# Middle stage of an audio tower kernel: dense products before every channel group, a third set of systems moved to the last stage, four stores moved to another queue

## What is computed

```python
# T: rows 0, 2, 4, ... of each segment of 256 rows -> 3 blocks of 128 tokens per sequence, attention in the block
scores = q @ k.T / 16;  h = softmax(scores) @ v            # q = k = v = the rows
# A: delta rule attention, 4 heads of 64, on h normalised
q, k, v = silu(conv4(x @ Wq)), silu(conv4(x @ Wk)), silu(conv4(x @ Wv))
T = inv(I + tril(kb @ k.T, -1))                            # unit triangular system per chunk
o_delta = chunkwise delta rule with T
fir_short, fir_long = causal filters of 3 and 63 taps over v, each channel with its own taps
o = gate-weighted mixture of fir_short, fir_long, o_delta and v;  h += rmsnorm(o) @ Wo
# F: 6 experts, 2 chosen per token by a router
h += sum_e weight_e * (gelu(LN(h) @ w1_e) @ w2_e)
```

## Time and profile before

| what | value |
|---|---|
| timed runs | median 2389.22 us of 3 (2379.17 to 2395.04) |
| the profiled execution | 2393.8 us, span from first to last instruction 2392.1 us |
| TensorE, VectorE, ScalarE, GpSimd busy | 94%, 77%, 54%, 23% of the span |
| mean granted clock of TensorE | 0.973 of full |
| steps of the last stage, one starting after the other | 47.53 us, with two columns solved in them or none |

### The profile page before, as it was taken

The page is one execution under the profiler, slowest core; times in us unless marked ns, Lnnn a source line. Parts: engine busy times, 40 slices in busy tenths (PEclk is TensorE's granted clock), DMA queues, the critical chain, the costliest instruction groups (busy, mean ns, idle before and its releaser), DMA issues.

```text
span 2392.1 us, 53303 instructions
## 1 busy us (share of the span) xinstructions
PE 2251.9 (94%) x20796; PEld 1635.1 (68%) x20796; DVE 1852.8 (77%) x5111; ACT 1290.8 (54%) x2632; POOL 555.5 (23%) x413
## 2 busy tenths in 40 slices
PE   5999999999799779999999999999999999999997
PEld 4666666666587666777677767776776677767765
DVE  4999999999868367677778777777777667767765
ACT  4888888888624334544454455445544544454452
POOL 1444444444400011121112111111111121112111
PEclk9999999999958879999999999999999999999999
DMA  3776777777778912233224222322233224222300
GB/s 98 231 245 229 229 241 245 236 238 236 247 241 314 378 60 71 71 108 96 78 70 139 91 77 71 125 81 74 70 132 105 71 70 133 77 71 76 125 21 21
DMA packets 224297, 334.44 MB, mean 140 GB/s; under 512 B 113870, under 2 KB 190766, under 8 KB 215342
## 3 DMA queue, kind: packets, MB, share of 16 engines
q1 hardware_dynamic: 219726, 309.01, 39.1%
q10 hardware_dynamic: 2304, 12.58, 1.3%
q0 software_dynamic: 2016, 9.44, 1.0%
HBM read 191.66 MB, written 164.23 MB: 149 GB/s over the span
## 4 chain that ended last, share of the span: by engine, by line
PE 49%; DVE 7%; ACT 6%; issue 4%; POOL 0%; DVEq 0%
PE bank L1662 7%; PE bank L1672 7%; PE bank L1595 6%; PE bank L1475 4%; PE bank L1555 4%; PE bank L1632 4%; PE bank L1571 2%; PE bank L1507 2%; PE bank L1543 2%; ACT L1808 2%; ACT L1803 2%; DVE v_all L2111 1%; PE bank L1503 1%; PE bank L1485 1%; DVE DL L2019 1%
## 5 line engine op out<-in xcount | busy, mean ns | idle before, releaser
L2111 DVE SCALAR_TENSOR_TENSOR v_all<-bank,we,v_all 128x256 f32<-128x256 f32 x576 | 264.9, 476 | 219.3 <-PE bank L1672 214.3
L739 DVE SCALAR_TENSOR_TENSOR Y<-bank,convw,Y 128x383 f32<-128x383 f32 (+2 forms) x576 | 330.6, 602 | 3.2 <-ACT Y L627 2.9
L1672 PE MATMUL bank<-w2e,HE 128*128 128x256 f32 x1152 | 327.9, 395 | 2.4 <-DVE v_all L2111 2.3
L1662 PE MATMUL bank<-v_all,w1e 128*128 128x384 f32 x768 | 289.6, 500 | 2.4 <-ACT HE L1808 2.3
L445 PE MATMUL bank<-pb,wqkv 128*128 128x384 f32 x768 | 282.4, 491 | 1.8 <-DVE Y L739 1.8
L1672 PEld LDWEIGHTS bank<-w2e,HE 128*128 128x128 f32 x1152 | 198.0, 191 | 55.3 <-issue 19.3
L1808 ACT ACTIVATE HE<-bank 128x384 f32<-128x384 f32 x192 | 94.1, 490 | 248.9 <-PE bank L1662 248.2
L1595 PE MATMUL bank<-v_all,w1g 128*128 128x384 f32 x512 | 193.4, 500 | 2.0
L1662 PEld LDWEIGHTS bank<-v_all,w1e 128*128 128x128 f32 x768 | 134.5, 191 | 75.9 <-issue 19.8
L445 PEld LDWEIGHTS bank<-pb,wqkv 128*128 128x128 f32 x768 | 132.1, 191 | 61.1 <-DVE Y L739 8.3
L1786 ACT ACTIVATE first_stage<-bank 32x384 f32<-32x384 f32 (+1 forms) x192 | 92.2, 480 | 135.7 <-PE bank L1583 119.2
(11 more groups left out here) (217 smaller groups left out, 5199.1 us busy)
## 6 DMA issues: line engine op xcount, KB each, us to landing
packa<-pa SPq DMA_DIRECT2D x32, 1932.0 KB, 6.2
v_all<-packa SPq DMA_DIRECT2D x32, 1932.0 KB, 8.1
packb<-pb SPq DMA_DIRECT2D x32, 768.0 KB, 6.1
v_all<-packb SPq DMA_DIRECT2D x32, 768.0 KB, 10.8
toeplitz<-taps SPq DMA_DIRECT2D x128, 190.0 KB, 5.3
toep<-toeplitz SPq DMA_DIRECT2D x32, 760.0 KB, 7.6
packb<-fsk SPq DMA_DIRECT2D x32, 384.0 KB, 2.7
first_stage<-fl SPq DMA_DIRECT2D x32, 384.0 KB, 8.7
```

Source lines behind the costliest of these rows:

```text
L739: dve.scalar_tensor_tensor(out=Y[:, j, lag:T], in0=proj_bank[j][:, 0:T - lag], scalar=convw[:, j, CK - 1 - lag:CK - lag], in1=Y[:, j, lag: ...
L1662: mm = pe.matmul(bank[6][:, 0:T], w1e[:, a, k, :], YT[s][:, a, :], start=(a == 0), stop=(a == HALF - 1))
L1672: pe.matmul(expert_bank(b), HE[k % 2][:, b * P:(b + 1) * P], w2e[:, k, :], start=True, stop=True)\
L2111: dve.scalar_tensor_tensor(out=HA[s][:, b, :], in0=expert_bank(b), scalar=we[s][:, b, k:k + 1], in1=HA[s][:, b, :], op0=ALU.mult, op1=ALU. ...
```

## The change

The calls of `dense` in the middle stage are laid otherwise: three at the start, four in front of group 0 behind the wait for its tile, three before groups 8, 16 and 24 as before, and one before every other group, ahead of the wait for its tile. Set 2 of the systems is not begun in the middle stage; in the last stage one column is solved right behind the transposed diagonal and two behind the last statistics, for set 2 in steps 0 to 9 and for set 3 in steps 10 to 19. GpSimd's loads of set 3 no longer wait for steps of set 2. The four stores of the last 64 channels are issued by SyncE at the start of the last stage, not by ScalarE at the end of the middle one.

```diff
-SPLIT = 20
+SOLVE_PASSES = (SC - 2) // 3
@@ middle stage, tensor
-                dense(5)
+                dense(3)
                 for i in range(0, groups // NT):
                     for s in range(NT):
                         it = i * NT + s
-                        if it and it % GI == 0:
-                            dense(3)
+                        if it:
+                            dense(1 if it % GI else 3)
                         pe.wait_ge(*toep_loaded[s].now(i))
+                        if it == 0:
+                            dense(4)
@@ middle stage, scalar
-                act.wait_ge(*fl_copied.now(NH * GI - 1))
-                for q in range(FQ):
-                    store(NH - 1, q)
                 act.wait_ge(setup_act, CLEARED)
@@ middle stage, gpsimd
-                load(3, 0, 2 * SOLVE_STEPS + 9)
-                load(3, 1, 2 * SOLVE_STEPS + 17)
-                load(3, 2, 2 * SOLVE_STEPS + 25)
+                for part in range(SG):
+                    load(3, part)
@@ middle stage, vector
-                solve["begin"](dve, 2)
-                for j in range(1, SPLIT):
-                    solve["column"](dve, 2, j)
@@ last stage, sync
+                def store_filtered(g, q):
+                    part = NB * BLK * DH // FQ
+                    sp.dma_start(dram["fl"][g][:, q * part:(q + 1) * part], stage[g][:, q * part:(q + 1) * part])\
+                        .then_inc(fl_stored[g], 16)
+
+                sp.wait_ge(*tail["fl_copied"].now(D // 8 - 1))
+                for q in range(FQ):
+                    store_filtered(NH - 1, q)
                 sp.wait_ge(fl_stored[2], 16 * FQ)
@@ last stage, vector
-                def columns_of(n):
-
-                    if n < 6:
-                        at = SPLIT + min(3 * n, 5 + n)
-                        return 2, at, at + (3 if n < 2 else 2 if n == 2 else 1)
-                    at = 1 + 2 * (n - 6)
-                    return 3, at, at + 2
-
-                def solve_columns(n):
...
+                def solve_first(n):
+                    if n < 2 * SOLVE_PASSES:
+                        g, turn = 2 + n // SOLVE_PASSES, n % SOLVE_PASSES
+                        if turn == 0:
+                            solve_begin(dve, g)
+                        solve_column(dve, g, 1 + 3 * turn)
+
+                def solve_others(n):
+                    if n < 2 * SOLVE_PASSES:
+                        g, turn = 2 + n // SOLVE_PASSES, n % SOLVE_PASSES
+                        solve_column(dve, g, 2 + 3 * turn)
+                        solve_column(dve, g, 3 + 3 * turn)
@@ step
                         transpose_diagonal(n, n % 2, 0, 0, n // 2).then_inc(tdiag_ready.sem, 1)
+                        solve_first(n)
                     if 0 <= f < NB:
                         add_expert(f, 4, 0)
@@ step
                         input_stats(n, 5)
-                        solve_columns(n)
+                        solve_others(n)
```

More of the change, by code:

```diff
@@ L2113, in add_expert @@
                         .then_inc(acc_done.sem, 1)
-                def columns_of(n):
-                    if n < 6:
-                        at = SPLIT + min(3 * n, 5 + n)
-                        return 2, at, at + (3 if n < 2 else 2 if n == 2 else 1)
-                    at = 1 + 2 * (n - 6)
-                    return 3, at, at + 2
-                def solve_columns(n):
-                    if n > 20:
-                        return
-                    g, first, last = columns_of(n)
-                    if first == 1:
-                        solve_begin(dve, g)
-                    for j in range(first, last):
-                        solve_column(dve, g, j)
+                def solve_first(n):
[9 more added lines that the diff above has]
+                        solve_column(dve, g, 3 + 3 * turn)
                 def step(i):
```

## The result

The changed kernel takes 2389.59 us (median of 20 runs, 2383.44 to 2396.75), the kernel before, timed beside it, 2378.89 (20 runs, 2375.91 to 2398.78). So two things were off: before is some 10 us faster than those three runs said, and the change makes it slower instead of faster. The profiled execution after took 2391.9 us (span 2390.2), the one before 2393.8 (2392.1): profile against profile the change looks 1.9 us faster. That contradiction is what this study is about.

The account below looks back on a forecast made before the run. The prediction took TensorE at half clock to bound the middle stage. Its terms, -4.0 (TensorE's end) - 4.4 (stage end) + 1.3 (solves) - 1.5 (step 0 clock) = -8.6 us, took 2389.2 to 2380.6; range 2366 to 2400.

Parts of the forecast that it names:

- Slow halves that go: Middle stage: 19 half groups and two triples of dense products return to full clock, -28.5 us.
- The change does less than it says: Rival, chance 0.06: the clock is not lost in every run before, so the median lands near 2389 us.
- The transfers end step 0: Rival, chance 0.14: full DMA engines land fl as before however early the meeting is, leaving 2387 us.
- Lost clock: Rival, chance 0.11: the clock falls in the first eight groups, single products do not raise it; +20, 2409 us.
- The start: Middle stage: four dense products behind the first load's wait are in the open, +4.9 us, bounds 3.4 and 6.7.
- The singles: Middle stage: one dense product ahead of every other group, 28 x 0.84 = +23.5 us on TensorE's path.
- Waits for loads: Middle stage: 5.9 us of later waits go and 2 us of new ones come, -3.9 us; the first load's 2.2 stay.
- TensorE's end: End of TensorE's middle-stage work: -4.0 us in sum, at 807.8 against 811.8 us.
- The end of the stage: Middle stage's end: four of ScalarE's five store issues move behind the engines' meeting, -4.4 us.
- cover of 3.0 us: Last stage's start: fl lands 17.8 us after the meeting, VectorE is free at 23.0, TensorE's first state comes at 26.0.
- Clock in step 0: Last stage's first step: after a shorter pause the clock stays up at first, -1.5 us, bounds 0 and -10.
- The solves: Last stage: 19 more columns on VectorE cost nothing except in step 2, +1.3 us, bounds 0 and 1.9.

Follow-up runs that it names:

- b_again: The kernel before, unchanged, run and profiled once more: 2381.65 us, ratio 1.0009.
- rest_only: The changed kernel with all dense products as before, so only the solves and the stores are moved: 2372.44 us, ratio 0.9981.
- stores_only: The kernel before with only the four last stores moved from ScalarE to SyncE, ahead of its loads: 2377.62 us, ratio 1.0016.
- x3_late: rest_only with GpSimd's three loads of the fourth systems group moved behind its first operation of the last stage: 2372.77 us, ratio 0.9963.
- rest_x3_fl: x3_late with SyncE's loads of fl ahead of those of the second chunk's packs and factors: 2368.1 us, ratio 0.9955.
- rest_step0: rest_only with three unused products behind the last group and five in the last stage's step 0: 2380.24 us, ratio 1.0006.
- after_fl: The changed kernel with SyncE's loads of fl first, no products in step 0: 2384.8 us, ratio 1.0039.
- the square: Four changed-kernel versions, fl behind packs and factors or first: 2389.6 and 2384.8 us without products in step 0, 2390.9 and 2381.5 with five.
- dense_only: The kernel before with only the change's dense products in the middle stage; solves and stores as before: 2390.87 us, ratio 1.0055.
- solves_only: The kernel before with only group 2 solved in the last stage and group 3's loads issued without waits: 2377.73 us, ratio 1.0009.
- after: The changed kernel itself, against the kernel before: 2389.59 us, ratio 1.0036.
- no_single: The changed kernel without the 28 single dense products, keeping the four behind the first wait: 2378.18 us, ratio 1.0.
- half_singles: The changed kernel with single dense products ahead of odd groups alone, 16 in place of 28: 2381.42 us, ratio 1.0024.
- nosingle_x3_fl_step0: The changed kernel without single products, fourth systems group loaded in the last stage, fl first, five products in step 0: 2370.45 us, ratio 0.9964.

## Why the prediction was wrong

**The step that failed is "Slow halves that go", -28.5 us.** Its arithmetic was right for the execution that was profiled, but that execution was a rare one. The sum also started from the median of three runs, 2389.2, where 20 runs give 2378.9. In b_again the part from the first dense product to the last Toeplitz product is 138.8 us and not 155.8. Its floor is 8.3 (start) + 32 x 3.31 + 3 x 2.52 = 121.8, and TensorE waited 6.0 for later loads; so half clock cost it 11.0 us, not 28.5. With that term the sum is -8.6 + 17.5 = +8.9, and the medians lie 10.7 apart (the profiled executions of the changed kernel and of b_again 6.4). Rest_only, stores_only, x3_late and rest_x3_fl have 130.4 to 131.6, so many executions lose less still. How often the long one comes: of 115 later runs of the kernel before, 16 were above 2389 us and 82 below 2380. Two profiles of such slow executions exist, the first one of before and rest_step0's, and both have the half clock through groups 0 to 7; the seven other profiles of kernels that start as before do not. That the others among the 16 have it too is argued, not shown. Their mean granted clock fits: 0.969 to 0.974, 0.9715 on average, where the 82 have 0.9802, which over 2385 us comes to some 41 us more at half clock (an estimate). But a mean does not say where: b_again's profile had 0.972 too, with its half clock elsewhere.

**Rivals.** "The change does less than it says", near 2389, is what happened as to its reason. That its number is met is luck: it meant no change against 2389.2, and what came is a loss of 10.7 against 2378.9. I gave it 0.06, though three runs 16 us apart, with the profiled one at the slow end of them, were in front of me. "The transfers end step 0" was right in that fl came too late, and wrong about why (below). "Lost clock" did not occur. The rule of the Trainium skill ("TensorE: Matmul & The Clock Gate", Part 1) would have put the sum at +12, close to the truth, but for another reason: the slow halves were mostly not there to be mended. Where the clock did fall at the start it stayed down for 48 us in both traces that show it, 45 of them unbroken Toeplitz work, against the rule; in rest_only it came back in such work (717.4 to 720.8), as the rule has it. So what the prediction read from one trace, that Toeplitz groups release nothing and dense products do, does not hold in every execution.

**What the products cost.** The start: +4.9 forecast, 5.0 measured, with the clock at half until 669.6, as assumed. The singles: 0.84 forecast, 0.81 measured. Waits for loads: 3.3 us in all, the first one alone, where 4.2 were expected. TensorE's end: 807.8 forecast, 806.8 measured (with a first product 1.6 us later than before's). So the changed kernel's middle stage was forecast within some 3 us; its error is all in what it was compared with.

**The end of the stage, -4.4.** The gap fell from 5.86 to 1.30. But stores_only gained nothing: GpSimd's loads and drain take ScalarE's place when the stage is short, and fl lands later. In the changed kernel the first of these two is hidden, as its stage is long, and the second is not.

**fl, and its cover of 3.0 us.** I counted bytes between meeting and landing and expected +17.8, with 22 as the bound. The forecast counted from the meeting; so counted it came at 829.75 - 807.8 = +21.9, which is +21.6 from the first product, and with the order turned round alone at 822.4 - 808.4 = +14.0 (after_fl). The bytes in flight were not the limit; SyncE's issuing was, 4.11 us for the stores and 8.92 for the factor loads, all ahead of fl. The landings of the stores show it: in the first profile of before the last one landed at 830.87 and fl was issued at 830.89; in the changed kernel it landed at 818.91, and fl was issued 4.7 us later. The rule of the Trainium skill that was cited ("DMA: Bandwidth & Descriptors", Issuing engines are not separate DMA queues) says that spreading DMAs over issuers saves only the time that a sequencer takes to issue them; I used it only for the queue that got rid of the stores, not for the one that took them. The price is not clear: TensorE idled 1.95 us for it in the trace, the square has 2 to 5 us, and the same change of order was worth 4.7 within one group in the kernel with before's dense products (rest_x3_fl against x3_late). It is of the order of what the move of the stores had won.

**Clock in step 0, -1.5.** It stayed up for the first two sets of products (1.13 us each in place of 2.08), as forecast. Then it was 0.50 until 861 us, for 48 us, where before's profile had 31. Both lengths occur in kernels of either kind: of the executions with step 0 mostly at half clock, five (the first profile, dense_only, rest_only, solves_only and, with fl first, after_fl) have it at 36.0 to 36.7 us, seven (b_again, after, no_single, stores_only, x3_late, half_singles and, with fl first, rest_x3_fl) at 40.3 to 43.8. In the five the clock was back 29 to 30 us after the first product, in the seven 43 to 55 us. What decides between them stays open. It also means that two single traces, such as those of after and after_fl, differ in step 0 by this as well as by their edit. The change did not make it better. Five products in step 0 did shorten it, from 40.9 to 37.6 us, but the time fell only with fl first.

**The solves, +1.3.** Solves_only shows none beyond its error of measurement: step 2 takes 44.7 us in it, 44.3 to 44.6 in the kernels without them, and the steady steps are 47.53. One thing stays open: the stores alone and the solves alone gain nothing (2377.6 and 2377.7, before 2376.3 beside them), the two together (rest_only) stand 4.7 us below before in another group, with an interval that holds 1.

## What to carry to other kernels

Before a repair is priced by one profiled execution, look at where that execution lies among the timed runs, and take a second profile: a clock history that costs 17 us in one run in seven is not worth 23 us of work in all of them. When issues move to another queue, price them twice, where they leave and in front of what they arrive. Work that only holds the clock belongs into time that is idle anyway. In the changed kernel it paid only when the next wait on the chain, here a transfer, had been moved out of the way first; beside rest_x3_fl it made no difference that the medians tell.

The best versions here are the kernel before's dense products with the systems group loaded in the last stage and fl first (2368.1 us, ratio 0.9955), with or without the five products in step 0. Where the rare long executions matter, the four dense products behind the first load's wait may be worth their 5 us, though one run in seven at 17.5 us is only 2.5 us on average: the eight kernels that have them, 84 runs, have none more than 8 us above their median, and seven of the eight kernels that start as before have one or two runs 11 to 25 us above it. Six of the eight have single products as well, so for the four alone stand only the 24 runs of no_single and nosingle_x3_fl_step0, where one in seven would be three runs.

## What the runs showed of the hardware

- GpSimd's drain at the end of a block lasts until its own transfers have landed: the last load of the systems landed at 795.86, 792.74, 786.18 and 781.26 us (solves_only, rest_only, after, no_single), and the drain ended at 796.48, 793.36, 786.80 and 781.88, 0.62 us later each time.
